# A decoder layer with routed experts on one core: blank rows written once, shared groups moved into the draining steps, transfers reordered

## The reference, cut to what matters

```python
# self attention; the mask multiplies, so later keys count with score 0
att = jnp.einsum('bhqe,bhke->bhqk', q, k) / jnp.sqrt(jnp.float32(he))
mask = jnp.tril(jnp.ones((c, c), dtype=att.dtype), k=-1)
att = jax.nn.softmax(att * mask, axis=-1)
...
# cross attention over the context
q = jnp.einsum('bsq,hq->bsh', query, W) + b
scores = jax.nn.softmax(jnp.einsum('bsh,bmh->bsm', q, info), axis=-1)
return jnp.einsum('bsm,bmh->bsh', scores, info)
...
# experts: each token goes to 2 of 8, and all go through a shared one (z)
h = jax.nn.silu(x @ w1.T) * (x @ w3.T)
...
z = _mlp(xt, sw1, sw2, sw3)
return (y + z).reshape(shape)
...
x = x + _L0_attn_ref(_layernorm(x, axis=-1), L0_attn_Wqkv, L0_attn_bqkv, L0_attn_Wr, L0_attn_br)
x = x + _L0_xattn_ref(_layernorm(x, axis=-1), ctx_1024, L0_xattn_W, L0_xattn_b)
x = x + _L0_ffn_ref(...)
```

## Time and profile before

| what | us |
|---|---|
| median of 3 runs (lowest, highest) | 789.51 (789.31, 791.03) |
| profiled execution, its own time | 788.71 |
| span of its profile | 787.0 |
| first scores (step 0) | 26.4 |
| one steady step | 31.9 to 32.5 |
| draining steps 17, 18, 19 | 22.7, 20.9, 14.9 |
| four shared groups | 613.4 to 634.9 |
| sorted stage | 634.9 to 744.4 |
| end: four shared groups, add-backs, output | 744.4 to 787.0 |

### The profile page before, as it was taken

One profiled execution on the slowest core, in us unless ns is written; L12 is line 12 of the kernel. 1 busy time (PEld: TensorE's weight loads), 2 busy tenths in 40 slices (PEclk: granted clock), 3 DMA queues, 4 the chain that ended last, 5 costly groups with the idle time before them and its releaser, 6 DMA issues.

```text
span 787.0 us, 17139 instructions
## 1 busy us (share of the span) xinstructions
PE 650.2 (83%) x5461; PEld 495.5 (63%) x5504; DVE 466.5 (59%) x1196; ACT 461.4 (59%) x1054; POOL 463.0 (59%) x780
## 2 busy tenths in 40 slices
PE   1546889989989899898998988989872789999872
PEld 0222456766766667676676766667761679889762
DVE  0234557687787877877878778755544333333226
ACT  3024647868668686686776867757642236666620
POOL 5124637577777776787777766766534416666630
PEclk9998779999999999999999999999996899999977
DMA  7335656846558475584774746835110212332183
GB/s 241 75 74 104 141 139 114 170 122 142 154 101 185 134 141 148 96 189 130 135 164 116 168 135 114 188 96 103 55 56 14 55 48 80 89 88 80 41 211 110
DMA packets 121414, 93.39 MB, mean 119 GB/s; under 512 B 9682, under 2 KB 112999, under 8 KB 121200
## 3 DMA queue, kind: packets, MB, share of 16 engines
q1 hardware_dynamic: 116976, 83.83, 46.5%
q0 software_dynamic: 4352, 8.47, 3.2%
HBM read 54.30 MB, written 38.08 MB: 117 GB/s over the span
## 4 chain that ended last, share of the span: by engine, by line
PE 53%; DVE 15%; DMA 11%; issue 6%; SPq 6%; POOL 4%; ACT 2%; another core or an unknown queue 0%; POOLq 0%; DVEq 0%; ACTq 0%
PE banks L949 8%; PE banks L292 6%; DMA info<-in_ctx 6%; PE banks L691 5%; DMA k_stack<-parts 4%; PE banks L314 4%; PE banks L243 3%; PE banks L911 3%; DVE mx L1267 3%; PE banks L931 3%; PE banks L701 3%; PE banks L731 2%; PE banks L303 2%; PE banks L254 2%; POOL sorted_rows L1600 2%
## 5 line engine op out<-in xcount | busy, mean ns | idle before, releaser
L1164 ACT ACTIVATE prob<-banks 128x512 f32<-128x512 f32 x192 | 115.4, 601 | 65.3 <-PE banks L694 64.2
L949 PE MATMUL banks<-info,xprobT 128*128 128x128 f32 (+1 forms) x832 | 106.6, 279 | 13.2 <-DMA info<-in_ctx 10.5
L1267 DVE TENSOR_REDUCE mx<-banks 128x2 f32<-128x512 f32 x128 | 87.9, 687 | 47.1 <-PE banks L701 45.4
L691 PE MATMUL banks<-kst,qst 48*128 48x128 bf16 (+1 forms) x512 | 79.6, 259 | 40.0 <-DMA qst<-q_parts 13.0
L949 PEld LDWEIGHTS banks<-info,xprobT 128*128 128x128 f32 (+1 forms) x832 | 98.5, 193 | 19.5 <-DMA info<-in_ctx 13.2
L1576 POOL TENSOR_SCALAR_AFFINE_SELECT prob<-prob 128x256 f32<-128x256 f32 (+1 forms) x192 | 91.0, 482 | 25.4 <-ACT prob L1164 25.2
L1600 POOL DMA_INDIRECT sorted_rows<-row,place x64 | 64.9, 1015 | 50.8 <-DVE place L1419 36.1
L1263 DVE TENSOR_REDUCE mx<-banks 128x4 f32<-128x512 f32 x64 | 44.0, 688 | 72.9 <-remote 40.6
L691 PEld LDWEIGHTS banks<-kst,qst 48*128 48x128 bf16 x512 | 30.0, 97 | 83.3 <-DVE mx L1267 24.7
L1055 ACT COPY xprobT<-banks 128x512 f32<-128x512 f32 (+2 forms) x128 | 64.6, 504 | 23.2 <-PE banks L931 23.2
L1296 DVE TENSOR_REDUCE xmax<-banks 128x1 f32<-128x896 f32 x64 | 62.4, 974 | 26.2 <-PE banks L911 19.4
(11 more groups left out here) (184 smaller groups left out, 1622.4 us busy)
## 6 DMA issues: line engine op xcount, KB each, us to landing
sorted_rows<-pad SPq DMA_DIRECT2D x33, 520.0 KB, 8.0
infoT<-in_ctxT SPq DMA_DIRECT2D x16, 800.5 KB, 6.7
info<-in_ctx SPq DMA_DIRECT2D x16, 448.0 KB, 4.9
kst<-k_stack SPq DMA_DIRECT2D x32, 192.0 KB
info<-in_ctx SPq DMA_DIRECT2D x16, 320.0 KB
q_parts<-parts SPq DMA_DIRECT2D x32, 96.0 KB, 2.7
k_stack<-parts SPq DMA_DIRECT2D x32, 96.0 KB, 2.8
qst<-q_parts SPq DMA_DIRECT2D x32, 96.0 KB
```

The costliest lines, as they stand in the source:

```text
L691: pe.matmul(alpha_bank[:, c * w:(c + 1) * w], lhsT=q[:, h, qs], rhs=k[:, h, keys], start=(c == 0), stop=False, skip_group_check=True)
L949: mm = pe.matmul(ps[:, V_BANK, u * P:(u + 1) * P], lhsT=xprobT[hf][0:w, m - blocks[0], :], rhs=info[0:w, m, :], start=(m == blocks[0]), st ...
L1164: act.activation(prob[n % 2][:, kind * 512:(kind + 1) * 512], ps[:, G_BANK, :], ACT.Exp, scale=SCALE).then_inc(s["p_exp"], 1)
L1267: dve.tensor_reduce(mx[:, 1, h:h + 2], bank.rearrange("p (c n) -> p c n", c=2), AX.X, ALU.max).then_inc(s["alpha_max"], 1)
```

## The change

- `blank_rows` goes. A region gets 384 more rows, and once the counts of 15 batches are known (`pad_at`, copied by VectorE in `places`), `blank_tails` writes 384 padding rows behind the last used row of each of the 8 regions, once, in step 19. Only `send_rows` of the last batch waits for them.
- EARLY is 6. The six groups are called inside steps 17, 18 and 19 (`early(i, n)`), two per step, both halves in banks 5 and 6. Two groups stay for the end, and their inputs are split ahead of the sorted stage.
- SP's step has another order: the second context half goes ahead of the transposed context; x in three pieces, w2 and the spare rows are queued in steps -2 to 2 (they stood at the start).
- The context is laid out with token 12p + m on partition p, so a half is one piece of 3584 or 2560 B per partition (the host permutes the transposed copy alike), and `home` numbers routed rows so that four of a partition lie together (2 KB).
- In step 0 alpha units alternate between banks 5 and 6. The four memsets of POOL's head come after the split of batch 0.
- Slots' table entries are read four at a time ahead of four loads. In the steps some calls have moved: VectorE's `gate_shift` ahead of `heads_out`, POOL's `cross_diff` ahead of `info_low(j, 0)`, ScalarE's `normalised2`, `gate_exp`, `cross_copy(k, 1, 1)`, TensorE's `xn2_T` and `cross_query`.

```diff
-REGION = B * S
+REGION = B * S + 3 * P
...
-EARLY = NGR // 2
+EARLY = NGR - 2
...
+        EARLY_BANKS = (5, 6)
...
+            def early_up(g, z):
+                if g is None:
+                    return
+                pe.wait_ge(s["x3_lo_done"], g + 1)
+                if 2 * g + z:
+                    pe.wait_ge(s["h_done"], 2 * g + z)
...
+                for half_w in range(2):
+                    w = slice(half_w * INTER + z * P, half_w * INTER + (z + 1) * P)
+                    for n, (a, b) in enumerate(((w13_hi, x3_hi), (w13_lo, x3_hi), (w13_hi, x3_lo))):
+                        mm = pe.matmul(ps[:, EARLY_BANKS[half_w], :], lhsT=a[:, E, w], rhs=b[g % 2], start=(n == 0), stop=(n == 2))
+                mm.then_inc(s["up_ps"], 1)
+
+            def early_down(g):
+                if g is None:
+                    return
+                pe.wait_ge(s["h_done"], 2 * g + 2)
+                if g:
+                    pe.wait_ge(s["shared_done"], g)
...
-                shared(0, EARLY)
                 pe.wait_ge(s["slots_done"], 1)
...
+        def early(i, n):
+
+            g = 2 * (i - B - 1) + n
+            return g if 0 <= g < EARLY else None
...
+        def bank_of(b, u):
+
+            return G_BANK if b == 0 and u % 2 else A_BANK
...
+            def later_inputs(i):
+
+                if i == -1:
+                    sp.dma_start(xall[:, 2 * T:4 * T, :], xt[:, 2 * T:4 * T, :]).then_inc(s["x_in"], 16)
...
+            def ctx_rows(b):
+
+                return ctx[b, 0:MF, :].rearrange("(p m) d -> p m d", p=P)
...
+            def blank_tails(l):
+
+                if l == B - 2:
+                    sp.wait_ge(s["pad_at_done"], 1)
+                    sp.wait_ge(s["pad_done"], 2)
+                    for e in range(E):
+                        at = sp.value_load(pad_at[0:1, e:e + 1], min_val=0, max_val=E * REGION - 3 * P)
+                        sp.dma_start(dsort[bass.ds(at, 3 * P), :].rearrange("(n p) r -> p n r", p=P),
+                                     pad[:].unsqueeze(1).to_broadcast([P, 3, ROW])).then_inc(s["blank_out"], 16)
...
             def step(i):
                 f, g, j, k, l = i + 1, i - 1, i - 2, i - 3, i - 4
-                load_w13(f)
+                write_parts(f, 0)
+                load_info(j, 0)
                 load_stack(f, 0)
                 write_maxima(i)
-                load_info(j, 0)
+                load_info(j, 1)
                 load_infoT(g)
                 write_parts(f, 1)
                 load_stack(f, 1)
-                blank_rows(i)
-                load_info(j, 1)
-                write_parts(f + 1, 0)
+                load_w13(f + 1)
+                blank_tails(l - 1)
+                later_inputs(f)
...
+                first = rows_at(0)
...
                 scores(i, 6)
+                early_up(early(i, 0), 0)
                 values(g, 1)
                 scores(i, 7)
                 gate_logits(i)
                 cross_transposes(k, 2, 0)
                 scores(i, 8)
+                early_up(early(i, 0), 1)
                 cross_scores(k, 3)
+                xn2_T(i)
+                early_up(early(i, 1), 0)
                 scores(i, 9)
                 cross_transposes(k, 2, 1)
-                xn2_T(i)
+                early_down(early(i, 0))
+                cross_query(j)
+                early_up(early(i, 1), 1)
                 cross_values(k, 1)
-                cross_query(j)
...
+                early_silu(early(i, 0), 0)
                 split_cast(f, 0)
+                cross_copy(k, 1, 1)
...
+                early_silu(early(i, 1), 0)
+                gate_exp(l)
...
+                early_hidden(early(i, 1), 0)
+                early_add(early(i, 0))
                 cross_min(k)
                 choices(l)
...
-            for n in range(2):
-                pool.memset(vaug[n][:], 1.0).then_inc(s["pads_done"], 1)
-                pool.memset(kst[n][:], 1.0).then_inc(s["pads_done"], 1)
...
+                cross_diff(k)
                 info_low(j, 0)
-                cross_diff(k)
+                residual(g)
                 cross_den(k)
                 masked(g, 9)
+                blank_stacks(f)
```

More of the change, by code:

```diff
@@ L357, in shared_hi, with early_hi, early_silu @@
                 act.copy(x3_hi[g % 2], x3T[:, g * GN:(g + 1) * GN]).then_inc(s["x3_hi_done"], 1)
+            def early_hi(g):
+                if g is not None:
+                    shared_hi(g)
+            def early_silu(g, z):
+                if g is not None:
+                    silu(g, z)
             def silu(g, z):
@@ L496, in rest @@
                         sorted_lo(q // 2 + 1)
-                shared(EARLY, NGR)
-                for g in range(NGR):
+                for g in range(EARLY, NGR):
+                    for z in range(2):
+                        hidden(g, z)
+                    if g > EARLY:
+                        add_shared(g - 1)
+                    if g >= EARLY + 2:
+                        add_back(2 * (g - EARLY - 2))
+                        add_back(2 * (g - EARLY - 2) + 1)
+                add_shared(NGR - 1)
+                for g in range(2 * (NGR - EARLY - 2), NGR):
                     add_back(g)
-            return rest
+            return early_hidden, early_add, rest
         def moe_pool(pool):
@@ L517, in rest @@
             def rest():
-                for g in range(2, EARLY):
+                for g in range(EARLY, EARLY + 2):
                     shared_lo(g)
@@ L1456, in step @@
                 cross_max(j, 2)
+                self_add(g)
+                alpha_max(f, 5)
+                statistics2(g)
+                alpha_max(f, 6)
+                early_add(early(i, 1))
+                alpha_max(f, 7)
+                early_hidden(early(f, 0), 0)
+                gate_shift(k)
             for i in STEPS:
```

188 lines of the change are left out of this document (103 added, 85 removed).

## The result

The changed kernel takes 802.46 us (median of 4 runs, 798.71 to 804.72) against 790.27 (4 runs) for the kernel before: ratio 1.0175, 95% interval 1.0137 to 1.0212. It is slower, by 1.4 to 2.1%; the forecast was 779.5 and faster.

| from ...

A forecast was written before the change was run, and what follows sets the result against it. TensorE was taken as bounding steady steps, with waits for the context half and VectorE; drain idle. 787.0 - 3.9 - 2.0 + 23.8 - 13.0 + 1.5 - 16.4 = 777.0; 778.7 with 1.7 outside, 779.5 on the median's scale; range 771 to 787, eight-in-ten 766 to 790.

The forecast's parts named there:

- The steady steps: One-batch steps: blank writes and the context-half wait go, -2.0 us in all, bounds -10 and +13.
- what moves is who waits. So I take 0: Steady steps: the minimum shortens, but VectorE's next small choice instructions are held until GpSimd's split ends; net 0.
- rival 3: Steady steps: second stack lands late, 1 us in each of 13 steps, context-wait gain unseen; 794.5 us, chance 0.14.
- The wait for the context half: Steady steps: TensorE's wait for the second context half, 1.19 us in the row shown, goes.
- The start: Steps 0 and 1: two banks in step 0 let step 1 start earlier, -3.9 us, bounds 0 and -6.
- The draining steps: Steps 17 to 19: six groups as chains, +7.9, +6.9 and +9.0, together +23.8 us; bounds +8 and +35.
- Rivals 1: Draining steps: the early groups hide almost fully, growth 8 us instead of 24; 763.5 us, chance 0.13.
- 2 (the steady steps gain): Steady steps: logit shift and minimum leave VectorE's chain, 0.8 us per step over 12 steps; 770 us, chance 0.15.
- 4: Draining-step chain: a ScalarE table change costs 1.28 us more than its row at five places; 786 us, chance 0.06.
- Ahead of the sorted stage: Last row writes to sorted stage: shared groups gone, slot table and loads remain; -13.0 us, bounds -9 and -18.
- the stage's low clock: Sorted stage: it begins at the low clock, as the shared stage did; +1.5 us.
- the end: Add-backs after the sorted stage: two groups left, loads bound it at 350 GB/s; -16.4 us.

The follow-up runs named there:

- e10: Changed kernel with the step's calls on TensorE, ScalarE, VectorE and GpSimd in the order of the kernel before; ratio to the kernel before 0.9946.
- e3: Kernel before with only three GpSimd calls in the changed order (difference of maxima, split, residual); 844.87 and 851.16 us in its two normal runs, against 829.98.
- e9: Changed kernel with GpSimd's split of 896 columns written as four instructions of 224; ratio to the kernel before 0.9866.
- e7: Changed kernel with SyncE's order of a step as in the kernel before; ratio to the kernel before 1.034.
- e1: Changed kernel with three GpSimd calls back (split's low half ahead of the difference of maxima, residual at the next step's head); ratio to the kernel before 1.0104.
- e13: Changed kernel with VectorE's calls of a step alone in the order of the kernel before; ratio to the kernel before 1.0399.
- e4: Changed kernel with one VectorE call moved, the maximum of unit 10 ahead of the choices; ratio to the kernel before 0.9913.
- e17: Changed kernel with routed rows numbered as in the kernel before (pieces of 512 B at the end); one run, 806.56 us.
- v18: Changed kernel, maximum of unit 10 first, no early groups in steps, two behind the last ranks, GpSimd's splits in four pieces; 763.66 us, ratio 0.9725.

## Why the forecast was wrong

- **The steady steps are the step that failed**, and in it the sentence "what moves is who waits. So I take 0". The mechanism was seen in the row (a minimum of 1.44 us that ends with GpSimd's split) and rightly said to move to the choices. But a hold is not a fixed sum handed on. It lasts as long as the part of GpSimd's instruction that is left when VectorE comes, once for each VectorE instruction while GpSimd has a next long one. The change put the residual's addition, which the working never names, right behind the split, and VectorE's arrival ahead of it. From the minimum to the maximum of unit 10 it takes 1.1 us longer, TensorE waits 2.3 us for this maximum instead of 1.2 (e10), and the clock falls in most steps: +14.1 where -2.0 was taken (e3, e9 and e10 show it). That is 16.1 of the 23.6 us by which the sum missed the span.
- I gave the new orders bounds only through other terms. The range of that term (-10 to +13) nearly held it, but its upper end came from SyncE's queue (rival 3), which e7 refutes, and the range given for the whole left it out.
- The wait for the context half went, as said, and brought nothing, not even the 2.0: the next thing late was VectorE's maximum, as the text had it, and the two waits had stood in for each other, 1.1 us per step in all.
- The start was right: step 1 begins at 50.09 (said: near 50), the stack load at 22.21 (said: 22.3).
- The draining steps: mechanism right, term too small, +29.5 for +23.8. Step 19 took +13.3 for +9.0: at 1.2 GHz the two halves took 4.5 us each where 3.9 and 3.5 stood, and the last up, the down and the add 7.0 where 4.0 stood. Steps 17 and 18, where no part was told apart, took +6.8 and +9.4 for +7.9 and +6.9. The range (+8 to +35) held it. Rivals 1 (they hide), 2 (the steady steps gain) and 4 are out: nine table loads from 571.51 to 640.65 take 1.28 us each, and behind eight of them the next instruction begins within 0.02 us.
- Ahead of the sorted stage -12.8 for -13.0, the stage's low clock +1.8 for +1.5, the end -14.4 for -16.4: these steps held. Half of the last gap is a slip of the sum: 24 transfers of 256 KB are 6.3 MB, not 6, which is 0.9 us at 350 GB/s.

## What to carry to other kernels

Where a tiny VectorE instruction takes over a microsecond and ends with a GpSimd instruction, the hold is part of VectorE's chain: its length changes with every move on either engine, so cost a reorder by laying both timelines side by side, and cut the long GpSimd instruction or put the work that others wait for (here the maximum) ahead of the small ones. Work moved into a gap pays only if its own chain fits there: two groups in the 16 us wait for rows and slot table cost about 1 us, six in the draining steps cost 29.5 us. And judge the orders of several engines together: moving back calls of one engine gave anything from -0.7% (e1) to +2.7% (e13) against the changed kernel, moving back those of four gave -1.8 to -2.3% (e10), all across groups of runs.

## What the runs showed of the hardware

The hold is per instruction: 2.71 us for two 128x8 instructions beside GpSimd instructions of 2.09 and 0.73, 1.26 beside quarters, 0.45 without; the minimum took 1.95 us where it came 0.15 us after the start of a split of 2.08, and 1.44 where it came 0.67 us after. VectorE's maxima that read the banks (0.69 us) were as long beside the split as elsewhere. The Trainium skill ("SBUF — State Buffer", section SBUF: two separate sides) says that the two engines share a pair of ports which an instruction of either locks until it ends, on VectorE one with two SBUF inputs, beside a GpSimd instruction that reads SBUF, among others; the trace agrees, with these numbers. TensorE's clock fell to 1.2 GHz in six of the eight steady steps between 255 and 522 us, 1 to 2 us after a wait of 2.3 us had ended, and came back 3 to 4 us later; in the other two the same wait was followed by no fall, and these steps lasted 32.7 and 33.0 us where the others up to 489 us lasted 33.3 to 33.7. In the kernel before, with waits of up to 1.5 us, and in e1, with waits of 1.8, it stayed at 2.4 GHz. And the same kernel took 786 to 790 us in two groups of runs and 830 to 845 in four others, by pauses that no row names. Whether that is a matter of the chip is not shown: the record gives chip 8 both for 829.98 (e1 to e4) and for 786.06 (e17, v18).
